# Last batch's hand-over to the experts: five pieces of work moved on VectorE, ScalarE and TensorE

## The reference

```
x = x + layernorm(attn(layernorm(x)))
x = x + layernorm(moe(layernorm(x)))

attn:  q, k = bf16(x Wq^T), bf16(x Wk^T), rotated (RoPE)
       s[i] = sum over j <= i of exp(q_i . k_j / 16)        # one number per row
       out  = relu(s fc1_w^T + fc1_b) fc2_w^T + fc2_b       # 1 -> 16 -> 256
moe:   logits = x gate_w + gate_b ; the top 2 of 8 experts, weights by softmax
       out = sum over the 2 experts of weight * (gelu(x W1e + b1e) W2e + b2e)   # 256 -> 1024 -> 256
```

## Time and profile before

| | |
|---|---|
| median of 3 runs | 636.11 us (635.61 to 638.78) |
| the profiled execution's own time | 634.63 us |
| its span in the trace | 632.8 us |
| TensorE matmul busy | 561.0 us, 89% |
| VectorE busy | 424.2 us, 67% |
| ScalarE busy | 365.8 us, 58% |
| GpSimd busy | 186.6 us, 29% |
| mean granted TensorE clock | 0.971 |

### The profile page before, as it was taken

How to read it: one execution, slowest core, us unless ns; L and a number is a source line. 1 busy time by engine, 2 the same in 40 slices (tenths; PEclk the granted TensorE clock), 3 DMA queues, 4 the chain that set the end, 5 groups by cost and what they waited for, 6 DMA issues and landing times.

```text
span 632.8 us, 14885 instructions
## 1 busy us (share of the span) xinstructions
PE 561.0 (89%) x4296; PEld 499.7 (79%) x4307; DVE 424.2 (67%) x1444; ACT 365.8 (58%) x836; POOL 186.6 (29%) x153
## 2 busy tenths in 40 slices
PE   1989898888799989999999999999999999999940
PEld 1747364553776989999999989999999999998940
DVE  5899798996988555555555556487388655455477
ACT  3367676674661744563654665685688563553572
POOL 2000045254436652332422322311412232422320
PEclk9989998989899989999999999999999999999985
DMA  8930011463207742232222352474374232222469
GB/s 220 363 117 2 0 68 68 135 225 103 77 35 218 223 90 42 50 50 50 42 42 50 51 167 53 67 248 83 46 237 100 52 51 50 42 41 50 117 170 328
DMA packets 51854, 66.80 MB, mean 106 GB/s; under 512 B 4870, under 2 KB 45292, under 8 KB 51692
## 3 DMA queue, kind: packets, MB, share of 16 engines
q1 hardware_dynamic: 37804, 47.87, 24.1%
q0 software_dynamic: 14016, 18.56, 16.9%
HBM read 38.26 MB, written 28.74 MB: 106 GB/s over the span
## 4 chain that ended last, share of the span: by engine, by line
PE 62%; DVE 25%; issue 5%; DMA 3%; ACT 2%; DVEq 1%; POOL 1%; SPq 0%; ACTq 0%; POOLq 0%
PE pY L1655 28%; PE pL L1643 24%; DMA sum_y<-y,dest 2%; PE pP L872 2%; DVE x_all L1090 2%; DVE z L1795 2%; PE pX L455 2%; DVE mstats L1023 2%; PE pS L786 2%; DVE xT_lo L979 1%; DVE qkr L994 1%; DVE rope_a L992 1%; PE pP L769 1%; POOL sum_y L533 1%; DVE rope_b L993 1%
## 5 line engine op out<-in xcount | busy, mean ns | idle before, releaser
L1578 ACT ACTIVATE h<-pL,b_now 128x256 f32<-128x256 f32 x272 | 112.3, 464 | 152.5 <-PE pL L1643 152.5
L533 POOL DMA_INDIRECT sum_y<-y,dest x68 | 110.9, 1630 | 268.5 <-DVE y L1699 245.9
L1655 PE MATMUL pY<-w_hi,h_lo 128*128 128x256 f32 x544 | 154.6, 284 | 3.1 <-DVE h_lo L1672 3.1
L1643 PE MATMUL pL<-xeT_hi,w_lo 128*128 128x256 f32 x544 | 151.5, 278 | 6.2 <-issue 5.8
L1672 DVE TENSOR_TENSOR h_lo<-h,h_hi 128x512 fp32r<-128x512 f32 x136 | 92.6, 691 | 88.2 <-ACT h_hi L1584 87.7
L1655 PE MATMUL pY<-w_hi,h_hi 128*128 128x256 f32 x544 | 151.5, 278 | 0.0
L1655 PE MATMUL pY<-w_lo,h_hi 128*128 128x256 f32 x544 | 151.3, 278 | 0.0
L1643 PE MATMUL pL<-xeT_lo,w_hi 128*128 128x256 f32 x544 | 150.8, 277 | 0.0
L1643 PE MATMUL pL<-xeT_hi,w_hi 128*128 128x256 f32 x544 | 150.7, 277 | 0.0
L1643 PEld LDWEIGHTS pL<-xeT_hi,w_lo 128*128 128x128 f32 x544 | 102.1, 188 | 7.5 <-issue 7.1
L1655 PEld LDWEIGHTS pY<-w_hi,h_lo 128*128 128x128 f32 x544 | 103.0, 189 | 4.5 <-DVE h_lo L1672 4.5
(11 more groups left out here) (296 smaller groups left out, 849.6 us busy)
## 6 DMA issues: line engine op xcount, KB each, us to landing
w_stage<-w SPq DMA_DIRECT2D x16, 1024.0 KB, 7.6
xt<-sorted_x SPq DMA_DIRECT2D x38, 260.0 KB, 2.7
sum_y<-fill SPq DMA_DIRECT2D x1, 4352.0 KB, 20.7
w_stage<-sum_y SPq DMA_DIRECT2D x8, 512.0 KB, 6.2
out<-z SPq DMA_DIRECT2D x8, 512.0 KB, 6.2
x_all<-x SPq DMA_DIRECT2D x3, 1024.0 KB, 8.4
sorted_x<-fill SPq DMA_DIRECT2D x8, 260.0 KB
sum_y<-y,dest POOLq DMA_INDIRECT x68, 3.9
```

Source lines behind the costliest of these rows:

```text
L533: pool.indirect_dma_start(out=sum_y, out_offset=bass.IndirectOffsetOnAxis(ap=to[:, i:i + 1], axis=0), in_=rows[:, i, :], in_offset=None, c ...
L1578: a = act.activation(h[:, c, :], pL[:, bk, i * TM:(i + 1) * TM], ACT.Gelu, bias=b1_now[par][:, c:c + 1])
L1643: mm = pe.matmul(pL[:, bk, i * TM:(i + 1) * TM], w[:, 0, col], x[:, k, :], start=(k == 0 and w is lo), stop=(k == KC - 1 and x is xeT_lo))
L1655: mm = pe.matmul(pY[:, i, 0:D], s[:, c, rows], w[:, 1, c * D:(c + 1) * D], start=(c == 0 and s is h_lo), stop=(c == FC - 1 and w is lo))
```

## The change

Five edits, all in the hand-written order:

1. VectorE: `hidden(3)` stands ahead of `place_rows(2)`, not behind it and tile 0's weights.
2. TensorE: `attention_mlp(3)` stands ahead of `turn_ahead(0)`; on ScalarE `take_hid` goes ahead of `turn_hi_ahead(0)`. The filler matmuls are 5 and 6, where they were 14 and 4.
3. VectorE: `stats_attn(3)` stands ahead of tile 0's low part, and `weigh_rows_ahead(0)` goes behind tile 1's low part.
4. VectorE: `order_experts` and `plan_order` stand ahead of `choose(3)`; the first was behind batch 2's placement, the second behind `choose(3)`.
5. The high part of the GELU output of tiles 0 and 1 is made by ScalarE (`high_inner_ahead`), not by VectorE.

```diff
+            def high_inner_ahead(g):
+
+                act.wait_ge(l2_done, 2 * g + ONE)
+                for bk in range(4):
+                    act.wait_ge(h_ready, 4 * g + bk + 1)
+                    act.activation(h_hi[:, 2 * bk:2 * bk + 2, :], h[:, 2 * bk:2 * bk + 2, :],
+                                   ACT.Copy).then_inc(h_hi_ready, 1)
...
             high_piece(act, 0, 0, 0, SPLITS - 1)
+            take_hid(B - 1)
             turn_hi_ahead(0)
-            take_hid(B - 1)
...
             square(B - 1, range(2, SQUARED))
+            high_inner_ahead(0)
             norm_high(B - 1, range(4, TB), last=True)
...
             inner_ahead(1)
+            high_inner_ahead(1)
...
-                keep_warm(pP[:, 0, :], 5 if j < B - 2 else 14)
+                keep_warm(pP[:, 0, :], 5)
+            attention_mlp(B - 1)
             turn_ahead(0)
-            keep_warm(pP[:, 0, :], 4)
-            attention_mlp(B - 1)
+            keep_warm(pP[:, 0, :], 6)
...
-                dve.wait_ge(h_ready, 4 * g + bk + 1)
-                dve.tensor_copy(h_hi[:, cs, :], h[:, cs, :]).then_inc(h_hi_ready, 1)
                 dve.wait_ge(h_hi_ready, 4 * g + bk + 1)
...
+            hidden(B - 1)
             place_rows(B - 2)
...
-            order_experts()
             save_tag(dve, 0)
-            weigh_rows_ahead(0, e0)
-            hidden(B - 1)
             split_ahead(range(3, SPLITS))
+            stats_attn(B - 1)
             lower_rows(dve, 0, pXa[0])
-            stats_attn(B - 1)
             aggregate_attn(B - 1)
...
                 lower_rows(dve, 1, pXa[1])
+                weigh_rows_ahead(0, e0)
                 save_tag(dve, 1)
...
             split_ahead(range(SPLITS, 2 * SPLITS))
+            order_experts()
+            plan_order()
             choose(B - 1)
-            plan_order()
             place_rows(B - 1)
```

## The result

The change made the kernel faster by half a per cent. 16 runs of the changed kernel have the median 633.56 us (630.86 to 637.70), 16 of the kernel before, taken with them, 637.12 us (633.41 to 640.41). The ratio is 0.9948 with a 95% interval of 0.9929 to 0.9968, which is 3.3 us less. A second measurement on another occasion gave 0.9957 (0.9933 to 0.9981), 2.7 us. The forecast was 3.8 us less.

A forecast was written before the change was run, and what follows sets the result against it. TensorE is full from 224.16 us; the landing of tile 1's output scatter decides when that starts. A 3.0 us lead plus 1.86 of clock, less a new wait, nets 3.8: 636.11 to 632.3 us, range 630.4 to 635.2.

The forecast's parts named there:

- parts 1 to 3: Up to tile 0's first layer: aggregate leads by 1.65 us; TensorE pauses 3.2 us there, losing 1.5 us of clock.
- A: The forecast itself, with 1.5 us lost to low clock behind tile 0's pause: 632.3 us (631.3 to 633.2), chance 0.50.
- B: The clock holds through the pause ahead of tile 0's first layer: leads 0.8 us more, 631.3 us, chance 0.20.
- parts 4 and 5: Up to the choice: ScalarE's casts cost 0, the tables end 0.45 us after the logits, the choice leads by 0.43.
- What is late next: After the choice: TensorE starts tile 1's second layer 1.45 us earlier; GpSimd leads by 3.0 us at 200.60.
- The sum: At tile 3's second layer: 3.0 us of lead plus 1.86 of clock, less a new wait: net 3.85, taken as 3.8.
- rival C: Tile 1's scatter stays held by SyncE's 2 MB of weights; GpSimd's lead shrinks to 1.45 to 2: 634.4 us, chance 0.17.
- the two waits of 1.24 and 0.66: TensorE's waits for tile 4's rows and `h_lo`, ahead of tile 3's second layer, were to shrink to about 0.4 to 0.6 us.
- the 1.86 us: Time lost at 1.2 GHz in tile 3's second layer (7.30 us against 5.44), to be regained at full clock.
- The new wait at tile 5's rows: TensorE, behind tile 3's second layer, would wait for tile 5's rows, giving back all but 0.85 of 1.86 us.
- D: TensorE stays at half clock from tile 0's first layer until the logits, costing some 10 us: 642 us, chance 0.06.
- E: Something between eats the leads, so they never reach 224 us: 636 us, chance 0.07.

The follow-up runs named there:

- late_weights: Changed kernel with SyncE holding an expert start's weights until the tile before its first one has landed in sum_y: ratio 1.0019 to the kernel before.
- plan_only: Kernel before with only order_experts and plan_order moved ahead of choose: ratio 0.9995.
- casts_only: Kernel before with only the high parts of tiles 0 and 1 made by ScalarE, not VectorE: ratio 0.9973.
- no_plan: Changed kernel with the move of order_experts and plan_order ahead of choose undone: ratio 0.9969 to the kernel before.
- no_casts: Changed kernel with VectorE making the high parts of tiles 0 and 1 again: ratio 0.9963 to the kernel before.
- mlp_only: Kernel before with only the moves of hidden, MLP, statistics and tile 0's weights, and the fillers: ratio 0.9979.
- late_fills: Changed kernel with SyncE's last four fills of region ends issued behind tile 3's load, not ahead of it: ratio 1.0025 to the kernel before.
- quiet_both: Changed kernel with SyncE's first weights and last four fills issued behind a later tile's load, at 237.5 us: ratio 0.9902 to the kernel before.

## Why the prediction was right, and which terms were off

**Statistics and pause (parts 1 to 3).** `hid` at 150.42 for 150.4, the aggregate 1.3 and 1.9 us earlier in the two profiles for 1.65: held. The pause ahead of tile 0's first layer is 3.42 us in the second profile for 3.2, with the clock at 0.50 behind it, as predicted. In the first, tile 0's rows came late (1.82 us of wait), the clock fell already on the fillers, and the layer itself ran at full clock. So A's loss occurred in the second profile; in the first the layer ran as B had it, but not for B's reason, since the clock did not hold, it fell and came back before the layer. The choice led by 0.29 and 1.07 us where A had 0.43 and B 0.8 more. That tile 0's rows come "as before" was true of one profile in two.

**Casts and tables (parts 4 and 5).** Held: the casts hid on ScalarE, and the choice follows the tables without idle time, since they and not the logits end last, as forecast.

**What is late next.** The wait for `gword` went, and GpSimd's first output scatter led by 3.85 us (first profile) and 3.05 (198.44 less 0.89, against 200.60) for 3.0: held.

**The sum.** Tile 3's second layer was to start 3.0 us earlier and did by 2.62 and 3.09. Those leads are 3.85 and 3.05 at the first output scatter, and shrank to 2.2 and 2.1 at tile 1's, by the wait for tile 0's scatter beside the fills, which the prediction did not have; the issue and landing of tile 1's scatter, quicker by about half a microsecond and by one, gave a part back. The mechanism of rival C was there in this form: the scatter took 8.21 and 7.78 us for 8.35, and late_weights showed that the weights make half of it. C's cut of the lead to 1.45 to 2 was not, since the scatter was issued sooner. But the pause and the low clock that C forecast came in the first profile, and there tile 4 began 1.43 us earlier than before, close to C's 1.7.

The term that failed is the pause: "the two waits of 1.24 and 0.66 shrink by 1.55". They did not. That took GpSimd's lead of 3.0 less TensorE's of 1.45, and TensorE's was mis-sized. It was 2.47 us ahead at the second layer of tile 1 (1.66 in the second profile), which is 1.0 and 0.2 above the 1.45, and 2.59 (1.80) at tile 2's first layer (202.79 against 199.10 + 1.10), and met no 1.15 us of wait for tile 3's rows. So it was 3.69 us ahead at tile 3's transposes (209.65 against 204.86 + 1.10), and 2.81 in the second profile. Its next two layers took 5.5 and 5.4 us where before they took 5.7 each, and it came to the pause 4.2 and 3.2 us ahead. The pause grew by 1.4 in the one and stayed in the other. I had not looked for the wait at 209.65, a wait between the two points at which I took leads.

**The clock.** The prediction itself names a low clock at 221 to 225 as a sign that it is wrong, and the first profile has it (0.51 from 219.50 to 226.40). The forecast of full clock rested on a pause of 0.4 to 0.6 us, and that pause did not come. In plan_only, where it is 0.61 us, the clock held (1.00 from 223.8 to 229.3):

```profile
223.79 0.38 PE L1655 MATMUL pY<-w_hi,h_lo 128*128 128x256 f32 x1 [0.61 <-DVE h_lo L1672]
```

The other profiles that have a pause there, with its length and what the 48 matmuls behind it took:

| profile | pause, us | layer, us |
|---|---|---|
| before | 1.90 | 7.30 |
| second of the changed kernel | 2.01 | 5.92 |
| casts_only | 2.10 | 7.44 |
| no_plan | 2.60 | 6.82 |
| no_casts | 3.20 | 7.30 |
| first of the changed kernel | 3.32 | 8.49 |
| mlp_only | 3.40 | 7.35 |
| late_weights | 4.17 | 6.30 |
| late_fills | 5.01 | 6.88 |

In eight of the nine the clock fell to its 1.2 GHz level for a part of the layer; it held only in the second profile, though the pause was no shorter than that of before. The Trainium skill (TensorE: Matmul & The Clock Gate, HAM oscillation — how this bites in real kernels) says that a long enough wait between bursts of matmuls sends the array back to its low clock; the rows agree in eight of these nine profiles. For a single execution the term is worth between −1.2 and +1.4 us, measured against the profile of before. If the low clock is the usual case before and after, as the table suggests, the 1.86 us are not gained and the gain is the lead at tile 3's second layer, 2.6 to 3.1 us, near the 3.3 and 2.7 that the runs measured. That is argued and not shown: of the runs without a profile no clock at this place is on record.

**The new wait at tile 5's rows** did not appear. In the second profile tile 3's second and tile 4's first layer took 5.92 and 5.65 us where the sum had twice 5.44 to 5.5, so TensorE came for the rows at 233.37, 4.66 behind the destinations of 228.71. The mechanism is shown by quiet_both: destinations at 225.09, rows at 229.96, 4.87 later for 4.86 forecast, and 0.81 us of wait.

So the number came out near in part by luck: the forecast was the lead of 3.0 with 1.86 us of clock added and 1.01 taken back by the new wait. The lead held, the clock's part came in one profile of two, and the wait in neither. D and E did not occur: nothing stayed at low clock, and in neither profile did the leads vanish before 224. What remains open is the split among edits 1 to 3 and 5, and what makes 48 matmuls take 5.44 us in one tile and 5.9 in another.

## What to carry to other kernels

Take the lead of each engine at every wait between the change and the point that sets the end, and not at two points: a wait in between that dissolves makes one engine early and turns up again at the next join. Where a large prefetch is issued beside a scatter that others wait for, its place is worth nearly as much as the reordering of the work (0.34% here against 0.5%); move it once, at the place where it hurts, since moving it in every tile cost 1.7%. And don't judge half a per cent by two profiled executions: the same kernel's two were 1.7 us apart. Lay them over each other at a point that the change can't move, and take the verdict from many runs.

## What the runs showed of the hardware

Beside 2 MB of weights on the hardware queue, GpSimd's scatter got next to nothing. From 206 to 209 us of the changed kernel the data went (packets, MB, share of 16 engines):

```profile
q1 hardware_dynamic: 237, 0.96, 82.6%
```

and in the same stretch of quiet_both, without weights:

```profile
q0 software_dynamic: 220, 0.21, 56.3%
```

The Trainium skill (DMA: Bandwidth & Descriptors, Queues, rings and completion order) has the engines take turns between queues, a packet at a time. The rows of before and after disagree, for 3 us each: GpSimd's queue has no row. From 208 to 211 us of the changed kernel it has packets again (135, 0.13 MB), beside the weights. The trace does not show which descriptors lay ready in a queue, so why it had none before that stays open. The price is 4.2 us for the scatter alone (late_weights) against 7.8 to 8.4 beside the weights. On one queue a row load behind the same weights took 8.46 us, and 2.82 us without them (quiet_both).
